# Linear attention in a four-layer block: the matrix engine's loop over batches written out

## The reference

```
q = phi(x @ W_Q.T); k = phi(x @ W_K.T); v = x @ W_V.T      # 8 heads of 64, phi(u) = elu(u) + 1
gamma = sigmoid(decay_log)
per token t:  S = gamma * S + k_t v_t^T;  z = gamma * z + k_t
              y_t = (S^T q_t) / (z . q_t + 1e-6)
gate = sigmoid(x @ W_g_w.T + W_g_b)
out = (y * gate) @ W_O.T
```

## Time and profile before

| what | value |
|---|---|
| three runs | 1882.28, 1885.28 (median), 1887.66 us |
| profiled execution | 1885.07 us |
| its span, first to last instruction | 1883.3 us |
| mean granted matrix clock | 0.995 |
| matrix engine busy | 1828.9 us, 97% |
| VectorE, ScalarE, GpSimd busy | 74%, 47%, 31% |
| linear attention | from about 818 to 1600 us |

### The profile page before, as it was taken

One profiled execution on the slowest core, in us unless ns is written; L12 is line 12 of the kernel. 1 busy time (PEld: TensorE's weight loads), 2 busy tenths in 40 slices (PEclk: granted clock), 3 DMA queues, 4 the chain that ended last, 5 costly groups with the idle time before them and its releaser, 6 DMA issues.

```text
span 1883.3 us, 37415 instructions
## 1 busy us (share of the span) xinstructions
PE 1828.9 (97%) x12929; PEld 1529.6 (81%) x12929; DVE 1394.4 (74%) x2679; ACT 880.3 (47%) x1717; POOL 592.0 (31%) x542
## 2 busy tenths in 40 slices
PE   8999999999999999989999999999999999999998
PEld 7888888888888888877777777878787877888887
DVE  6566566556668888778777878787878788888885
ACT  6656656665654444443333333333333332444443
POOL 5313203211332222233433333434343334522211
PEclk9999999999999999999999999999999999999999
DMA  7100000000022122120000000000000001222332
GB/s 246 43 1 0 0 0 0 0 0 0 13 48 59 29 33 31 28 63 13 13 12 12 11 11 11 11 11 11 11 11 11 12 12 22 40 58 63 64 59 54
DMA packets 230631, 53.21 MB, mean 28 GB/s; under 512 B 209696, under 2 KB 228768, under 8 KB 230176
## 3 DMA queue, kind: packets, MB, share of 16 engines
q1 hardware_dynamic: 229296, 49.53, 13.0%
q10 hardware_dynamic: 1264, 2.76, 0.4%
HBM read 18.69 MB, written 8.39 MB: 14 GB/s over the span
## 4 chain that ended last, share of the span: by engine, by line
PE 70%; DVE 14%; issue 7%; POOL 4%; ACT 2%; SPq 1%; DMA 1%; DVEq 0%; ACTq 0%; POOLq 0%
PE PS L1212 16%; PE PS L1221 9%; PE PS L331 8%; PE PS L870 7%; PE PS L841 6%; PE PS L340 5%; PE PS L1750 3%; PE PS L859 3%; PE PS L1729 3%; PE PS L881 2%; PE PS L1679 2%; PE PS L1717 2%; DVE lin_zq L1515 2%; SPq L270 1%; PE PS L1740 1%
## 5 line engine op out<-in xcount | busy, mean ns | idle before, releaser
L331 PE MATMUL PS<-ln_xh,lin_w 128*128 128x512 f32 x768 | 249.9, 394 | 3.8 <-DVE lin_kT L1498 2.7
L1144 ACT ACTIVATE ff_silu<-PS 128x512 f32<-128x512 f32 x192 | 114.4, 597 | 235.5 <-PE PS L1212 207.3
L1179 DVE SCALAR_TENSOR_TENSOR ff_h<-PS,ff_silu 128x512 f32<-128x512 f32 x192 | 131.2, 684 | 113.1 <-PE PS L1212 99.3
L331 PEld LDWEIGHTS PS<-ln_xh,lin_w 128*128 128x128 f32 x768 | 145.2, 189 | 40.5 <-DVE lin_kT L1498 8.7
L577 POOL TENSOR_TENSOR qk<-qk,swapped 64x128 f32<-64x128 f32 (+2 forms) x96 | 96.9, 1010 | 240.1 <-DVE swapped L721 234.3
L1163 DVE TENSOR_TENSOR ff_h_lo<-ff_h,ff_h_hi 128x512 fp32r<-128x512 f32 x192 | 165.0, 860 | 0.4
L870 PE MATMUL PS<-probT,v_a 128*128 128x128 f32 x1152 | 153.3, 278 | 0.0
L870 PEld LDWEIGHTS PS<-probT,v_a 128*128 128x128 f32 x1152 | 139.5, 192 | 14.3 <-ACT probT L641 7.4
L331 PE MATMUL PS<-ln_xl,lin_w 128*128 128x512 f32 x384 | 150.7, 393 | 0.0
L841 PE MATMUL PS<-qk 128*128 128x512 f32 (+3 forms) x384 | 145.2, 489 | 0.9 <-POOL qk L577 0.9
L166 POOL TENSOR_SCALAR ln_var_eps<-ln_mean_var 128x4 f32<-128x4 f32 x64 | 15.5, 242 | 401.9 <-DVE ln_mean_var L139 401.9
(11 more groups left out here) (191 smaller groups left out, 5325.1 us busy)
## 6 DMA issues: line engine op xcount, KB each, us to landing
ff_raw<-ln_xn SPq DMA_DIRECT2D x464, 32.0 KB, 2.0
ln_xl<-ln_xn SPq DMA_DIRECT2D x288, 32.0 KB, 2.0
out_x<-X SPq DMA_DIRECT2D x15, 512.0 KB, 2.9
X<-in_x SPq DMA_DIRECT2D x7, 1024.0 KB, 5.4
stage<-in_w_lin SPq DMA_DIRECT2D x1, 2048.0 KB, 8.4
stage<-in_w_gate SPq DMA_DIRECT2D x2, 768.0 KB, 7.3
stage<-in_w_up SPq DMA_DIRECT2D x2, 768.0 KB, 8.7
stage<-in_w_down SPq DMA_DIRECT2D x2, 768.0 KB, 10.1
```

What stands on the lines that cost most here:

```text
L331: last = nc.tensor.matmul(out, w, x, start=n == 0, stop=n == len(terms) - 1)
L1144: nc.scalar.activation(silu[:, f % NB_GU, :], PS[:, f % NB_GU, :], ACT.Silu, scale=W_SCALE).then_inc(silu_done.sem, 1)
L1179: nc.vector.scalar_tensor_tensor(h[:, f % 2, :], PS[:, NB_GU + f % NB_GU, :], W_SCALE, silu[:, f % NB_GU, :], ALU.mult, ALU.mult).then_inc ...
```

## The change

In the matrix engine's program of the linear phase the call of `run_batches` is replaced by a Python loop over the eight batches, so that each batch's instructions are written out with constant semaphore values. The other four engines keep their loops, and what is computed is the same.

```
-            run_batches(pe, turn)
+            for b in range(NB):
+                turn(b, b == 0, b == NB - 1)
             return rest_of_last
```

## The result

| | before | after |
|---|---|---|
| median | 1885.28 us | 1900.0 us |
| runs | 1881.33 to 1887.66 (5) | 1897.86 to 1902.43 (5) |
| profiled execution, its span | 1885.07, 1883.3 us | 1900.0, 1898.2 us |

The ratio is 1.0082, with a 95% interval of 1.0064 to 1.01: slower by 0.8%, the side that was forecast, but 1 us beyond the range. The forecast had been 8 us of loss; it was 15.

A forecast was written before the change was run, and what follows sets the result against it. The matrix engine, busy 97% of the span, was taken as the bound. Late moves from code fetches, 5.8 us (3.6 second halves, 2.2 first), plus 2.4 us of clock falls made 8.2 us, so 1893 us; range 1884.5 to 1899 us.

The forecast's parts named there:

- Removed branch and registers: Matrix engine's linear-phase loop: dropping six branches and the register instructions gains 0, with -8.8 us as the far end.
- 30 packets more: Instruction queue q8: straight code fetches 6 packets a batch in batches 2 to 6, about 71 packets in all.
- Fetches delay the moves, the moves delay L1435, L1435 delays L1750: Each linear-phase half: packets share DMA engines with SyncE's 16 moves; the matrix engine's last output product waits, 5.8 us in all.
- The size of the lateness: Batches 2 to 6: second halves lose 0.73 us each, 3.6 us; first halves 1.08 us in two of five, 2.2 us.
- The upper bound: Batches 2 to 6: at most five first turns and five clock falls, 5 x (1.99 + 1.58) = 17.9 us, 1903 us.
- The clock: Ends of new batches: 1.5 of five fall to 1.2 GHz after long idle, 1.58 us each, 2.4 us; present fall stays.
- Hidden fetches: Rival for batches 2 to 6: fetches are hidden and batches stay at 95.5 us, 1885 to 1887 us; chance 0.27.
- A gain from straight code: Rival for the linear-phase loop: branches and register instructions did cost time, 1876 us, or 1881 us for half; chance 0.05.
- The first turn in every batch, with the clock: Rival for batches 2 to 6: each behaves like the first turn and brings the clock down, 1903 us; chance 0.10.

The follow-up runs named there:

- the divided moves: SyncE issues 8 of each half's 16 block moves, ScalarE's queue the other 8; 1872.9 us on the kernel before (loop), 1871.8 us with batches written out.
- the new order: ScalarE's high part goes behind chunk 1's gated_high, GpSimd's L1435 before the blocks' low part; 1880.22 us on the kernel before (loop), 1882.21 us written out.

## Why the prediction was wrong

- **Removed branch and registers: nothing.** Right. The gaps of the matrix engine's weight loads with no releaser have the same sums before and after in batches 3 to 6 (L1679 8.4, L1717 7.2, L340 6.7 us), and the divided moves give 94.66 us with and without a loop.
- **30 packets more, fetched in batches 2 to 6, without holding the matrix engine.** Right: 32 more, and the same sums as above say that the matrix engine does not wait for its code there.
- **Fetches delay the moves, the moves delay L1435, L1435 delays L1750.** Right in each link, shown by the chain and by removing the link (15 us of loss become 2 with the new order, and none with the divided moves). Why a code packet delays a move is not shown.
- **The size of the lateness: this step failed.** The prediction put second halves at 0.73 us each, 3.6 us, and first halves at 1.08 in two of five, 2.2 us. Measured between the marks over 95.5 us a batch, without the clock, the second halves lost 7.1 us and the first halves 4.6. The number of first halves that are hit hard was right, two (batches 4 and 5), but they lost 1.3 and 2.2 us. For second halves no such case was counted, and two came: batches 3 and 4 lost 2.7 and 1.7 us there. I had taken the lateness of the second halves from two rows, both of halves in which no code packet met the last moves: in batch 1 the last one starts 7.5 us after the first issue, in batch 0 one starts after 1.9 us and one only after 12.1 us, when the moves have ended. The first half of batch 1 was the row to read: two packets, the second at 10.6 us, and 1.52 us late. I had taken it for the large case and for a matter of first halves; four of the ten new halves, two of them second halves, were 1.68 to 2.67 us late (14.46, 13.78, 13.47 and 14.43 us from the first issue to ScalarE, against 11.79).
- **A reading that hid it.** The prediction calls SyncE's 10.42 us the issues "and their landing". The row ends with the last issue; ScalarE starts 1.37 us later. In two of the four late halves the issue was only 1.06 and 0.73 us longer and the landing 2.67 and 1.99 us late, so the issue stretch, which I had used for the lateness of batch 7, can understate what happens to the last landing.
- **The upper bound.** "At most five first turns" was no bound: the first turn had idled 1.84 us at its end, and the same batch, straight code now but with its code fetched as before, idled 2.89 us in the run after, batch 3 3.60 us. One execution of one turn isn't the worst case of a collision in time. The 18 us of that bound cover the 15 measured, but not because its terms were right.
- **The clock.** 2.4 us forecast for 1.5 falls. Beside the fall inside batch 7 that both executions have, three stand in batches 2 to 7 where one stood before, 3.2 us more. The fall at the end of batch 1, which the prediction kept in its place, is gone. That the length of the idle decides was wrong: after 2.89 us at the end of batch 1 the clock stayed at 2.4 GHz, after 1.99 us at the end of batch 2 it fell to 1.2 GHz. These are the stretches behind the two (columns as the earlier trace rows):

```profile
1013.40:1016.80 3.40, 3.40 (x21) 3.07 (x22) 1.12 (x2) 0.84 (x2) 2.09 (x2) 1.00 0.00 0
...
1110.90:1114.30 3.40, 3.40 (x15) 3.11 (x14) 0.76 (x2) 0.63 (x1) 1.23 (x2) 0.51 0.00 0
```

- **Rivals.** Hidden fetches: out. A gain from straight code: out. The first turn in every batch, with the clock, 1903 us, was the nearest number, but by luck: batches 2 to 6 took 96.9 to 100.1 us and not 99.1 each, and two of the five had a fall of the clock, not all.

## What to carry to other kernels

A loop whose body stays loaded, as this one of 6 code packets, need not cost anything at its back edge, and writing it out turns its code into DMA traffic in every pass; look who waits for small transfers at that time, and give those slack first. When a loss comes from collisions in time, one observed pass is a sample: look where in the wait each packet fell, and price the case in which it falls at the end. Measure lateness where the waiter starts, not where the issuer ends. The 16 transfers that one queue issued in 10.4 us were issued by two in 5.5 us; that alone gained 10 us with the loop and left nothing of the 15 us that writing the loop out had cost.

## What the runs showed of the hardware that was not expected

- A taken back edge of the matrix engine's sequencer took 0.2 us with a body of 6 code packets, and 3.5 and 3.9 us with one of 12.
- The last 32 KB move of a set, which met a code packet, took 3.6 us to land instead of 2.0; two transfers of 16 KB that were cut into 64 packets delayed a set of 16 moves by 0.2 us in all.
- An idle of 2.89 us left the granted clock alone in one place, and one of 1.99 us was followed by 3.4 us at half of it in another.
- 64 waits of the matrix engine on constants, one behind the other, came out as 32 instructions in the trace.
